# Attention stage of a hyperbolic transformer layer: q and k transposed by a DMA in place of TensorE, and VectorE's order around it

## What is computed

```python
xm = expmap0(layer_norm(logmap0(x)) * (1 + sc_msa) + sh_msa)
q, k, v = (_to_heads(plin(xm, w, b)) for w, b in ...)     # 16 heads of 16, each scaled by its own norm
scores = einsum('bhqd,bhkd->bhqk', logmap0(q), logmap0(k)) / 4
out_h = expmap0(softmax(scores) @ logmap0(v))
attn_out = plin(_from_heads(out_h), w_o, b_o)
x = mobius_add(x, expmap0(g_msa * logmap0(attn_out)))
# then the same with a two-layer MLP, and the input is added
```

## Time and profile before

| | us |
|---|---|
| median of 3 runs | 842.89 |
| lowest and highest | 840.26 and 843.83 |
| the profiled execution's own time | 841.73 |
| its span in the profile | 839.9 |
| attention stage, from about 60 to 550 | some 490 |
| PE busy | 703.7 (84%) |
| DVE busy | 673.6 (80%) |
| ACT busy | 586.5 (70%) |
| POOL busy | 353.3 (42%) |

### The profile page before, as it was taken

One profiled execution on the slowest core, in us unless ns is written; L12 is line 12 of the kernel. 1 busy time (PEld: TensorE's weight loads), 2 busy tenths in 40 slices (PEclk: granted clock), 3 DMA queues, 4 the chain that ended last, 5 costly groups with the idle time before them and its releaser, 6 DMA issues.

```text
span 839.9 us, 29703 instructions
## 1 busy us (share of the span) xinstructions
PE 703.7 (84%) x9393; PEld 515.0 (61%) x9393; DVE 673.6 (80%) x2231; ACT 586.5 (70%) x1627; POOL 353.3 (42%) x682
## 2 busy tenths in 40 slices
PE   5967999999999999999999999731868899889986
PEld 2756777777777777777777777520325555556555
DVE  3868888888888888888888888757797888888885
ACT  1125777777777777777777777633577888888874
POOL 1005555556555565555555565401232333233231
PEclk9979999999999999999999999955899999999999
DMA  9931111111111111111111110021343545455432
GB/s 324 354 86 52 51 52 51 56 56 46 50 54 56 56 43 51 56 56 52 44 54 56 55 46 27 23 66 51 88 116 98 148 137 144 126 150 151 138 102 100
DMA packets 51811, 73.99 MB, mean 88 GB/s; under 512 B 7081, under 2 KB 34609, under 8 KB 51762
## 3 DMA queue, kind: packets, MB, share of 16 engines
q1 hardware_dynamic: 49970, 70.55, 28.4%
q10 hardware_dynamic: 1792, 2.89, 0.9%
HBM read 64.24 MB, written 9.18 MB: 87 GB/s over the span
## 4 chain that ended last, share of the span: by engine, by line
PE 44%; DVE 25%; issue 14%; DMA 5%; ACT 4%; SPq 3%; DVEq 2%; POOL 2%; POOLq 0%; ACTq 0%
PE p_qkv L893 21%; PE p_oz L867 8%; DVE u L1156 7%; PE p_s L958 3%; PE p_s L883 3%; DMA mod_b<-mod_rows 3%; SPq L365 2%; DVE g_all L1191 2%; PE p_qkv L958 2%; PE p_oz L861 2%; DMA x_all<-in_x 2%; DVEq L50 2%; PE p_t L944 1%; DVE qk L1231 1%; PE p_o L972 1%
## 5 line engine op out<-in xcount | busy, mean ns | idle before, releaser
L893 PE MATMUL p_qkv<-wqkv,tT 128*128 128x256 f32 x768 | 194.3, 390 | 26.6 <-DVE u L1156 26.3
L893 PEld LDWEIGHTS p_qkv<-wqkv,tT 128*128 128x128 f32 x768 | 135.1, 192 | 57.4 <-issue 23.8
L477 POOL TENSOR_TENSOR qk<-qk 128x512 f16<-128x512 f32 x64 | 73.9, 1155 | 142.0 <-ACT qk L613 142.0
L907 PEld LDWEIGHTS p_o<-v,pT 64*64 64x64 f32 x4096 | 68.3, 136 | 36.1 <-issue 36.1
L1184 DVE TENSOR_TENSOR z<-p_oz,bo 128x256 f32<-128x256 f32 x64 | 27.1, 424 | 77.5 <-PE p_oz L867 77.3
L618 ACT ACTIVATE qkT<-p_s 128x1024 f32<-128x1024 f32 x64 | 65.5, 1023 | 31.1 <-PE p_s L850 31.1
L907 PE MATMUL p_o<-v,pT 64*64 64x17 f32 x4096 | 72.8, 209 | 12.0 <-ACT pT L663 12.0
L663 ACT ACTIVATE pT<-p_s 128x1024 f32<-128x1024 f32 x64 | 65.4, 1022 | 20.3 <-PE p_s L883 20.3
L867 PE MATMUL p_oz<-wo,oT 128*128 128x256 f32 x256 | 75.2, 418 | 0.6 <-ACT oT L623 0.5
L850 PE MATMUL p_s<-ident,qk 128*128 128x128 f16 x1024 | 67.9, 219 | 6.7 <-issue 4.5
L1222 DVE TENSOR_TENSOR qk<-u,fac 128x256 f32<-128x256 f32 x128 | 70.3, 588 | 0.1
(11 more groups left out here) (268 smaller groups left out, 1758.0 us busy)
## 6 DMA issues: line engine op xcount, KB each, us to landing
mod<-mod_rows SPq DMA_DIRECT2D x128, 128.0 KB, 2.8
x_all<-in_x SPq DMA_DIRECT2D x8, 1024.0 KB, 13.9
gate<-mod_rows SPq DMA_DIRECT2D x128, 64.0 KB, 2.5
mod<-mod_rows SPq DMA_DIRECT2D x32, 256.0 KB, 4.1
mod_b<-mod_rows SPq DMA_DIRECT2D x32, 256.0 KB, 4.1
out<-x_all SPq DMA_DIRECT2D x32, 256.0 KB, 2.2
gate<-gate_rows SPq DMA_DIRECT2D x32, 128.0 KB, 3.5
bqkv<-gate_rows SPq DMA_DIRECT2D x32, 128.0 KB, 3.8
```

Of the source, the lines that this page charges most:

```text
L477: pool.tensor_tensor(low, qk[:, :].rearrange("p (a h d) -> p a h d", a=2, d=HD), qk4[:, :, :, 0, :], ALU.subtract).then_inc(low_ready, 1)
L893: mm = pe.matmul(p_qkv[:, a * D:a * D + D], tT[:, k, c, :], wqkv[:, c, a * D:a * D + D], start=c == 0, stop=c == C - 1)
L907: mm = pe.matmul(p_o[S * e:S * e + S, col:col + VW], pT[keys, e, g, :], v[keys, k, 2 * g + e, :], start=True, stop=True, skip_group_check= ...
```

## The change

The sixteen transposes on PE, their copy by ACT and the fp16 identity go. In their place SP issues one transposing DMA per tile from `qk4` (128 partitions by 2048 fp16, 512 KB) to `qkT`. `qk4` gets a second buffer in the space of `mod_b`, which only the MLP stage uses otherwise; `bias_left` moves from there to `xa`. The steps that write `qk4` wait until the DMA of the tile two before has landed. The DMA waits for the repeats and for the scores of the tile before (which read `qkT`). PE waits for its landing where it waited for `qkT` before.

`project` moves from the start of slot D to slot C, the slot whose `qkv` it reads. `gate_z`, `dot_x`, the second half of `square_z` and `keep_stats` move to a new step G with lag 7, so that the stage has one slot more, and `st` gets a second column set. DVE's second part is now: gate, clip, dot, project, repeats, bias sum. On POOL `token_root` comes ahead of `low_parts`.

```diff
+        qk4s = (qk4[:, :, :, :, :], mod_b[:, :, :].rearrange("p j n -> p (j n)").bitcast(F16).rearrange(
+            "p (a h r d) -> p a h r d", a=2, h=H, r=4))
...
-        L_A, L_B, L_C, L_D, L_E, L_H, L_L = 0, 1, 2, 3, 4, 5, 6
+        L_A, L_B, L_C, L_D, L_E, L_H, L_L, L_G = 0, 1, 2, 3, 4, 5, 6, 7
...
                 if on(h, off, L_H):
                     i, k = 2 * h + off - L_H, (off - L_H) % 2
+                    sp.wait_ge(again_ready, 2 * i + 2)
+                    after(sp, s_psum, i)
+                    sp.sem_inc(rows_begun, 1)
+                    sp.dma_start(qkT[:, :, :, :].rearrange("p a g n -> p (a g) n"),
+                                 qk4s[k].rearrange("p a h r d -> p (a h r d)"), transpose=True).then_inc(qkT_in, 16)
                     after(sp, zg_ready, i - 1)
...
             def high_parts(i, k):
                 act.wait_ge(qk_ready, 2 * i + 2)
-                after(act, qkT_psum, i)
-                after(act, low_ready, i)
-                after(act, again_ready, 2 * i)
+                after(act, qkT_in, 16 * (i - 1))
...
-            def evac_qkT(i):
-                act.wait_ge(qkT_psum, i + 1)
-                after(act, s_psum, i)
-                act.activation(qkT[:, :, :, :].rearrange("p a g n -> p (a g n)").bitcast(F32), p_s[:, :], ACT.Copy).then_inc(qkT_ready, 1)
...
-            def transpose_qk(i):
-                pe.wait_ge(again_ready, 2 * i + 2)
-                after(pe, p_ready, i)
-                for a in range(2):
-                    for g in range(G):
-                        mm = pe.transpose(p_qkT[:, a, g, :], qk4[:, a, 2 * g:2 * g + 2, :, :].rearrange("p h r d -> p (h r d)"),
-                                          ident16[:, :])
-                mm.then_inc(qkT_psum, 1)
...
             def scores_wait(i):
-                pe.wait_ge(qkT_ready, i + 1)
+                pe.wait_ge(qkT_in, 16 * i + 16)
+                after(pe, p_ready, i)
...
             def slot_until_rows(h, off):
-                if on(h, off, L_D):
-                    project(2 * h + off - L_D, (off - L_D) % 2)
...
             def slot_from_bias(h, off):
+                if on(h, off, L_G):
+                    gate_z(2 * h + off - L_G, (off - L_G) % 2, h + (off - L_G) // 2)
+                if on(h, off, L_C):
+                    clip_t(2 * h + off - L_C, (off - L_C) % 2)
+                if on(h, off, L_G):
+                    dot_x(2 * h + off - L_G, (off - L_G) % 2)
+                if on(h, off, L_C):
+                    project(2 * h + off - L_C, (off - L_C) % 2)
+                if on(h, off, L_E):
+                    repeat_parts(2 * h + off - L_E, (off - L_E) % 2)
                 if on(h, off, L_L):
                     add_bo(2 * h + off - L_L)
-                if on(h, off, L_E):
-                    repeat_parts(2 * h + off - L_E)
-                if on(h, off, L_L):
-                    gate_z(2 * h + off - L_L, (off - L_L) % 2, h + (off - L_L) // 2)
-                if on(h, off, L_C):
-                    clip_t(2 * h + off - L_C, (off - L_C) % 2)
-                if on(h, off, L_L):
-                    dot_x(2 * h + off - L_L)
```

More of the change, by code:

```diff
@@ L181, in build @@
         t2s = pT[:, :, :, :].rearrange("p e g n -> p (e g n)").rearrange("p (k j d) -> p k j d", k=2, j=2)
-        bias_left = mod_b[:, 0, :]
+        bias_left = xa[:, :, :].rearrange("p j d -> p (j d)")
         ss2 = sb("ss2", [P, 2])
@@ L325, in run_tiles @@
         def run_tiles(eng, slot):
-            run_slots(eng, slot, FIRST, T, T + L_L)
+            run_slots(eng, slot, FIRST, T, T + L_G)
         def run_pairs(eng, slot):
@@ L469, in scale_v, with low_parts, keep_stats @@
                                    fac[:, 2 * H:3 * H].unsqueeze(2).broadcast_to([P, H, HD]), ALU.mult).then_inc(v_ready, 1)
-            def low_parts(i):
+            def low_parts(i, k):
                 pool.wait_ge(high_ready, i + 1)
                 pool.wait_ge(qk_ready, 2 * i + 2)
-                after(pool, qkT_psum, i)
-                low = bass.AP(qk4[:, :, :, :, :].tensor, 2 * HD, [[8 * H * HD, P], [4 * H * HD - HD, 2], [4 * HD, H], [1, HD]])
-                pool.tensor_tensor(low, qk[:, :].rearrange("p (a h d) -> p a h d", a=2, d=HD), qk4[:, :, :, 0, :],
+                after(pool, qkT_in, 16 * (i - 1))
+                big = qk4s[k]
+                low = bass.AP(big.tensor, big.offset + 2 * HD, [[8 * H * HD, P], [4 * H * HD - HD, 2], [4 * HD, H], [1, HD]])
+                pool.tensor_tensor(low, qk[:, :].rearrange("p (a h d) -> p a h d", a=2, d=HD), big[:, :, :, 0, :],
                                    ALU.subtract).then_inc(low_ready, 1)
-            def keep_stats(i):
+            def keep_stats(i, k):
                 pool.wait_ge(z_squared, i + 1)
@@ L488, in slot @@
                     scale_v(2 * h + off - L_E, (off - L_E) % 2)
-                    low_parts(2 * h + off - L_E)
                 if on(h, off, L_C):
                     token_root(2 * h + off - L_C, (off - L_C) % 2)
+                if on(h, off, L_E):
+                    low_parts(2 * h + off - L_E, (off - L_E) % 2)
                 if on(h, off, L_D):
                     head_roots(2 * h + off - L_D)
-                if on(h, off, L_L):
-                    keep_stats(2 * h + off - L_L)
+                if on(h, off, L_G):
+                    keep_stats(2 * h + off - L_G, (off - L_G) % 2)
             run_tiles(pool, slot)
@@ L648, in inverse_norms, with square_z, square_zg @@
                 act.activation(y0[:, :], lnh[:, :], ACT.Exp, scale=-0.5).then_inc(y0_ready, 1)
-            def square_z(i):
+            def square_z(i, k):
                 act.wait_ge(z_ready, i + 1)
-                after(act, stats_kept, i)
+                after(act, stats_kept, i - 1)
                 after(act, z_squared, i)
-                act.activation(junk[:, 1, :], z[:, :], ACT.Square, accum_out=st[:, 0:1]).then_inc(z_squared, 1)
+                act.activation(junk[:, 1, :], z[:, :], ACT.Square, accum_out=st[:, k, 0:1]).then_inc(z_squared, 1)
+            def square_zg(i, k):
                 act.wait_ge(zg_ready, i + 1)
@@ L657, in square_z @@
                 act.activation(junk[:, 2, :], g_all[:, bass.ds(i, 1), :].rearrange("p a d -> p (a d)"),
[L658 removed]
+                               ACT.Square, accum_out=st[:, k, 3:4]).then_inc(zg_squared, 1)
             def exp_scores(i):
@@ L675, in slot @@
                 if on(h, off, L_E):
-                    high_parts(2 * h + off - L_E)
+                    high_parts(2 * h + off - L_E, (off - L_E) % 2)
                 if on(h, off, L_H):
@@ L913, in slot @@
                     pe.wait_ge(ffw_made, 8)
-                if on(h, off, L_H):
-                    transpose_qk(2 * h + off - L_H)
                 if on(h, off, L_B):
@@ L1223, in scale_qk, with repeat_parts @@
                                       fac[:, a * H:a * H + H].unsqueeze(2).broadcast_to([P, H, HD]), ALU.mult).then_inc(qk_ready, 1)
-            def repeat_parts(i):
+            def repeat_parts(i, k):
                 dve.wait_ge(high_ready, i + 1)
                 dve.wait_ge(low_ready, i + 1)
-                after(dve, qkT_psum, i)
-                q4, k4 = (qk4[:, a, :, :, :].rearrange("p h (y z) d -> p h y z d", y=2) for a in range(2))
+                after(dve, qkT_in, 16 * (i - 1))
+                q4, k4 = (qk4s[k][:, a, :, :, :].rearrange("p h (y z) d -> p h y z d", y=2) for a in range(2))
                 dve.tensor_copy(q4[:, :, :, 1, :], q4[:, :, :, 0, :]).then_inc(again_ready, 1)
```

35 lines of the change are left out of this document (16 added, 19 removed).

## The result

Against 843.36 us for the kernel before (median of 4, 840.26 to 844.5) the changed kernel takes 936.85 us (median of 4, 936.74 to 942.93). The ratio is 1.113 with a 95% interval of 1.108 to 1.118: 94 us slower. The profiled execution is the slowest of the four, 942.93, its span 941.1, so that its slots are read a little long.

The account below looks back on a forecast made before the run. Today a DVE and PE ring (`u`, `qkv`, `project_o`, bias sum) bounds at 7.55 us a slot; with the DMA 8.68, so 1.13 more in 62 slots, +70.1, and 1.3 at the end: 914 us, range 830 to 1045.

Parts of the forecast that it names:

- The new wait: PE waits ahead of the last part of `qkv` until the DMA lands, 1.5 to 2.5 us in each slot.
- the second ring: Exponential, roots on ACT and POOL, `rlim` and `o` on DVE, `qkv` and scores on PE: 7.43 us a slot.
- X: Time from SP's issue of the transposing DMA to its landing, taken as 5 us.
- The upper end: Highest price of the DMA's landing, from 128 packets per engine at 76 ns plus 1.2 us of start: 11 us.
- its own formula: A slot of the attention loop takes (12.36 + X) / 2, 8.68 us with X at 5.
- The two-slot ring: Landing, last `qkv` part, scores, exponential, `rlim`, DVE's first part, gate's product, SP's loads, next DMA: 12.36 us plus X.
- a rival with 0.14: PE's clock falls, coming and going: a slot of 10.1 us and 1002 us in all; chance 0.14.
- SP's way from the gate's product: SP issues the `gate` and `mod` pairs after the product, then reaches the transposing DMA: 3.19 us.
- the "floor" of 7.43: Shortest slot without any DMA, set by the ring from exponential through `rlim`, `o`, `qkv` and scores: 7.43 us.
- the second sum that I did for X under 2.6: If the DMA lands in 2.6 us or less, 7.33 to 7.48 us a slot, 830 us at best; chance 0.15.
- The prediction's last sign: The forecast is wrong at the root if the slot grows though the landing is under 3 us.
- 14 us at the most: Largest gain the change could give, 62 slots at 0.22 us each.

Follow-up runs that it names:

- experiment 5: The changed kernel with eight transposes of the identity on PE ahead of its wait for the landing; 919.5 us.
- experiment 8: A plain 32 KB copy in place of the transposing DMA, q and k untransposed: in the changed kernel 868.6 us, in its tuned version 826.6 us.
- experiment 2: The changed kernel with PE's transposes back and gate loads one slot later, 894.1 us; with loop's end and high parts also moved, 890.7 us.
- experiment 7: The changed kernel, DMA kept, with gate loads later, PE's wait behind the last `qkv` part, loop's end and high parts moved; 867.5 us.
- experiments 1 and 9: The changed kernel with PE's transposes and ACT's copy back, no DMA, 893.7 us; the changed kernel with DVE's old order, DMA kept, 906.6 us.
- experiment 10: The kernel before, transposes on PE, with `u` made ahead of the gate's product and the dot; 858.5 us.

## Why the prediction was right, and what its sum left out

**The sign and the mechanism.** The new wait is the one that was named: ahead of the last part of `qkv`, by the DMA, none by `u`; with it came DVE's waits for the roots and for `u`. Where it occurs it is 1.6 us (58.0 / 37), as forecast, but in three slots of four, not in each, so 1.2 us a slot; and there were 44 slots in 400 us, not 46 to 47. PE's waits for `o`, named as the sign of the second ring, came besides. 914 was forecast and 936.9 came.

**The price of X.** Taken as 5, measured 4.4 (4.2 to 5.7). The estimate by the nearest load was close, in part by luck: a load of rows shows nothing of turning or of small packets. The upper end was far off: the packets cost (0.456 x 941.1 - 0.284 x 839.9) x 16 / 133,120 = 23 ns each, not the mean of 76 that the earlier trace rows gave for packets of 1.4 KB; and the 1.2 us of start in it stands in no row (the store of 256 KB leaves 2.2 - 0.8 = 1.4). The plain copy was put at 3.0 and took 3.4. The rule that a transposing DMA is as fast as a regular one (the Trainium skill, Advanced Engine Details and Errata, X-Bar Transpose) doesn't hold here: 4.4 against 3.4 us for the same 512 KB, and 93.5 against 73.0 us of loss. Nor does the price of 1309 ns taken per block (the Trainium skill, VectorE: DVE Perf Modes, The three transpose paths): sixteen blocks landed in 4.4 us.

**The sum came near by errors against each other.** With X = 4.4 its own formula gives (12.36 + 4.4) / 2 = 8.38 us a slot and 896 us, so X was 18 us too much and the rest 41 us too little. That the forecast was 23 us off and not 41 is luck. The two-slot ring itself is in the trace (first row from the chain that ended last: start, us to landing; landing to PE, 350.05, and `rlim`, 356.21, are in the slot shown above):

```profile
345.53 4.47 DMA qkT<-qk
...
352.75 1.02 ACT L665 ACTIVATE pT<-p_s 128x1024 f32<-128x1024 f32 x1 [4.22 <-PE p_s L875]
...
360.74 0.43 DVE L1180 SCALAR_TENSOR_TENSOR g_all<-z,gate 128x256 f32 x1 [0.48 <-issue]
...
364.21 2.48 SPq L387 DMA_TRANSPOSE qkT<-qk  x1
```

The DMA 4.47, landing to exponential 2.75 (predicted 1.57; at half speed), exponential to `rlim` 3.46 (3.88), `rlim` to the gate's product 4.53 (3.72; 0.48 of it the jump back), product to DMA 3.47 (3.19): 18.68 us for the two slots, where the formula with this X has 16.83. The missing 41 us are:

- *The clock.* It was a rival with 0.14, at the price of halfway between full and half speed. It came, in part: 0.84 to 0.90 by stretches of 100 us, and is worth some 14 us (experiment 5). The rival and the forecast weren't alternatives: the wait that I forecast was itself the gap that lowers the clock. The Trainium skill (TensorE: Matmul & The Clock Gate, HAM oscillation) describes a kernel whose PE waits for a transfer in each tile and whose clock falls by it; the trace agrees, 0.87 with the gap and 1.00 with it filled.
- *The loads' ring.* The prediction had SP's way from the gate's product as 3.19 us; it is 4.0 on the mean, since the product itself is stretched (see below), SP's pairs start 1.8 us apart in place of 1.4 in every second slot (so they did before: 312.40 and 314.10 against 304.74 and 306.09, and only the shorter was read), and 0.2 to 0.3 us lie between the last pair and the transposing DMA. In the formula 0.8 us more over two slots are 25 us. Nor did the prediction see that the `mod` loads hang on the same product, just ahead of `lnx`. That ring gives 8.0 us a slot where the copy lands in 2.2 (experiment 8), more than the "floor" of 7.43. So the second sum that I did for X under 2.6, that the second ring bounds and 830 us at best come of it, was wrong: at about 2 us of landing the changed kernel takes 868.6. The prediction's last sign, "wrong at the root if the slot grows though the landing is under 3 us", is met by that kernel: the landing was the larger part of the loss, but the change as made was slower without it too.
- *The loop's end.* `slot_from_bias` now begins with the gate's product instead of the bias sum, whose wait of 1.1 us hid the jump back. It costs 0.49 us (11.7 / 24) every other slot, in the path to SP.
- *DVE's products under POOL's low parts.* The prediction looked at who waits for the low parts and put their place at no cost; it did not look at who runs beside them. Nor is it `token_root` that moves them: they begin when ACT's high parts are there, for which POOL waits in 42 of 48 slots (78.8 us). What moved is DVE's own order. Before, they ran from 302.11 to 303.26, while DVE waited for `project_o`; now they meet `t` or the gate's product, whose mean from 120 to 560 us went from 450 to 803 ns (the longest 1361).

How the 41 us divide among the four can't be read off. Mended alone were the clock's gap (14 us) and the loads' ring (27), besides them the place of PE's wait (32); the last two never were, and with the transposes on PE both together gave 3 (experiment 2). The place of the wait, the loads and the last two together give 65 (experiment 7), the clock's gap with them.

**The gain.** That the change can give 14 us at the most came near in number, not in cause: 12.6 us (839.2 to 826.6) with the landing almost gone and only in the mended order, and the bound is DVE, its `t` stretched, at 7.27 us a slot and not the second ring at 7.33 to 7.53. For the order as it was changed it is wrong: that kernel loses 29.4 us even so.

## What to carry to other kernels

In a kernel like this, moving a transpose from PE to a DMA can pay only if its landing lies outside every ring of waits; no run here shows it paying (the best still loses 28 us). What helped: put the wait for it last, ahead of the first instruction that reads the data, and fill or avoid the gap on PE, whose clock is lost with it. When an order is changed, follow each queue that the moved step releases (here SP's loads, one slot ahead) and each engine that runs beside it, not only those that wait for it; a step that covered a jump, a hand-over or another engine's work takes that cover with it. And try such an order together with its mending: half of it alone (experiments 1 and 9) tells little of what the whole can do.

## What the runs showed of the hardware that was not expected

- A DVE product of two SBUF operands that meets a POOL operation on SBUF of 1.15 us almost stops. `t` in experiment 8 is one example; this is another: issued 0.08 us behind it at 368.45 the gate's product took 1.36 us and ended 0.29 behind its end, where alone it takes 0.41. A reduction that ran beside one of the same kind (348.41, with POOL from 348.78) kept its 0.95 us. In the changed kernel:

```profile
368.37 1.15 POOL L483 TENSOR_TENSOR mod_b<-qk,mod_b 128x512 f16<-128x512 f32 x1 [1.53 <-ACT mod_b L618]
368.45 1.36 DVE L1180 SCALAR_TENSOR_TENSOR g_all<-z,gate 128x256 f32 x1
```

  The Trainium skill (SBUF — State Buffer, Who interferes with whom) says that a DVE instruction with two SBUF inputs contends with one of GpSimd that reads SBUF, and calls the ports that they share an exclusive lock. The trace agrees: DVE, which came second, ended 0.27 and 0.29 us behind POOL.
- A transposing DMA holds the queue that issues it: 1.7 to 3.1 us on SP for one in the changed kernel, 2.5 on the median (1.7 and 1.9 in experiment 7), where a plain one takes 0.5 and two 1.16.
- A DVE instruction that waits for the semaphore of the one ahead of it on the same engine starts 0.32 us late (experiment 10); with the dot between the two, as before, nothing was lost.
